# Gathered token rows turned on VectorE and moved within SBUF, in place of TensorE transposes

## The reference, cut to what matters

```python
x = x + attention(layernorm(x), ctx)            # 32 heads, 8 groups; not touched
h = layernorm(x).reshape(T, 512)                 # T = 8 * 256 = 2048 tokens
logits = h @ gate_w.T                            # 32 experts, the best 4 of each token
cw[t, sel] = softmax weights of the best 4, normed to 1
g = einsum('th,ehi->eti', h, Wg); u = einsum('th,ehi->eti', h, Wu)
a = silu(g) * u * cw.T[:, :, None]
large = einsum('eti,eih->th', a, Wd)             # inner width 192
small = the same with cWg, cWu, cWd: 16 chunks, inner width 128, chunk = expert // 2
out = x + large + 0.05 * small
```

## Time and profile before

| | |
|---|---|
| median of 3 runs | 1080.85 us |
| profiled execution, its own time | 1079.25 us |
| its span | 1077.5 us |
| TensorE busy | 1005.4 us (93%) |
| ScalarE / VectorE / GpSimd busy | 374.5 / 415.3 / 298.5 us |
| expert stage, first gather to the end | 458.8 to 1077.5 us |
| one slot in it, start to start | 7.65 us |
| DMA engines busy in it | 65 to 70% |

### The profile page before, as it was taken

The page is one execution under the profiler, slowest core; times in us unless marked ns, Lnnn a source line. Parts: engine busy times, 40 slices in busy tenths (PEclk is TensorE's granted clock), DMA queues, the critical chain, the costliest instruction groups (busy, mean ns, idle before and its releaser), DMA issues.

```text
span 1077.5 us, 18627 instructions
## 1 busy us (share of the span) xinstructions
PE 1005.4 (93%) x5447; PEld 651.7 (60%) x5448; DVE 415.3 (39%) x1065; ACT 374.5 (35%) x730; POOL 298.5 (28%) x395
## 2 busy tenths in 40 slices
PE   8889999999999877279999999999999999999995
PEld 6566667666665534156666666666666666666662
DVE  5587777777776627711111111111111111111110
ACT  2255454554555637812122222222222222222221
POOL 3011101011020002123434343433343434343442
PEclk9899999999999988579999999999999999999998
DMA  6163324243231118017566676766676677667433
GB/s 215 39 159 94 80 58 110 72 105 87 68 94 44 41 67 335 10 44 224 150 157 186 191 214 165 211 164 208 157 203 171 150 225 214 160 155 219 80 61 60
DMA packets 51755, 146.68 MB, mean 136 GB/s; under 512 B 9856, under 2 KB 19200, under 8 KB 47360
## 3 DMA queue, kind: packets, MB, share of 16 engines
q1 hardware_dynamic: 32016, 103.11, 29.1%
q0 software_dynamic: 17632, 42.74, 20.3%
q10 hardware_dynamic: 2064, 0.26, 0.2%
HBM read 100.73 MB, written 29.36 MB: 121 GB/s over the span
## 4 chain that ended last, share of the span: by engine, by line
PE 55%; DMA 1%; issue 0%; ACT 0%; POOL 0%; DVE 0%; POOLq 0%; ACTq 0%
PE y_ps L1564 18%; PE g_ps L1547 16%; PE u_ps L1547 16%; PE xt_ps L1540 3%; PE at_ps L1556 2%; DMA out_x<-yb,yidx 0%; DMA xg<-xd,gidx 0%; POOL out_x L1451 0%; ACT yb L1483 0%; ACT xT L1472 0%; ACT sg L1476 0%; DVE a L1518 0%; DVE a L1519 0%; POOL gidx L1434 0%; POOLq L1458 0%
## 5 line engine op out<-in xcount | busy, mean ns | idle before, releaser
L1564 PE MATMUL y_ps<-W,aT 128*128 x468 | 213.8, 593 | 0.8 <-DVE aT L1505 0.8
L1451 POOL DMA_INDIRECT out_x<-yb,yidx x78 | 125.3, 1606 | 296.0 <-DMA out_x<-yb,yidx 120.2
L397 ACT ACTIVATE pt<-stp 128x512 f32<-128x512 f32 x256 | 139.1, 596 | 145.2 <-PE stp L723 144.4
L518 DVE TENSOR_REDUCE mx<-s 128x2 f32<-128x512 f32 x256 | 163.7, 682 | 59.5 <-PE s L709 58.8
L1547 PE MATMUL g_ps<-W,xT 128*128 x624 | 183.2, 437 | 0.9 <-ACT xT L1472 0.9
L1547 PE MATMUL u_ps<-W,xT 128*128 x624 | 181.0, 433 | 0.0
L1547 PEld LDWEIGHTS u_ps<-W,xT 128*128 128x128 f32 x624 | 118.9, 191 | 49.8 <-issue 0.6
L1518 DVE TENSOR_TENSOR a<-u_ps,sg 128x192 f32<-128x192 f32 x78 | 27.9, 358 | 291.1 <-ACT sg L1476 291.1
L1476 ACT ACTIVATE sg<-g_ps 128x320 f32<-128x320 f32 x78 | 34.1, 437 | 305.0 <-PE u_ps L1547 305.0
L1547 PEld LDWEIGHTS g_ps<-W,xT 128*128 128x128 f32 x624 | 113.5, 192 | 39.0 <-issue 2.4
L1564 PEld LDWEIGHTS y_ps<-W,aT 128*128 128x128 f32 x468 | 82.8, 190 | 75.6 <-issue 75.6
(11 more groups left out here) (188 smaller groups left out, 929.8 us busy)
## 6 DMA issues: line engine op xcount, KB each, us to landing
W<-in_wts SPq DMA_DIRECT2D x32, 2048.0 KB, 8.1
qst<-q SPq DMA_DIRECT2D x42, 256.0 KB, 5.0
xs<-in_x SPq DMA_DIRECT2D x8, 512.0 KB, 3.7
ctxT<-in_ctx SPq DMA_DIRECT2D x8, 512.0 KB, 4.1
out_x<-xs SPq DMA_DIRECT2D x16, 256.0 KB, 2.2
kst<-k SPq DMA_DIRECT2D x48, 64.0 KB, 2.1
xd<-xs SPq DMA_DIRECT2D x11, 256.0 KB, 2.6
qst<-nm SPq DMA_DIRECT2D x128, 2.0 KB
```

The source lines that it names most:

```text
L397: act.activation(pt[g % 2][:, 2 * (j % 2) + r, :, :], stp[n % STP][:, :, :], ACT.Exp, scale=DH ** -0.5).then_inc(exp_done, 1)
L518: dve.tensor_reduce(mx[j // CH % 2][:, h:2 * G:G], s1[r][:, :, :], AX.X, ALU.max)\
L1451: pool.indirect_dma_start(out[:, :], bass.IndirectOffsetOnAxis(yidx[p][:, :], 0), yb[p][:, :], None, compute_op=ALU.add).then_inc(y_added, ...
L1564: m = pe.matmul(y_ps[:, :], aT[p][:, c, :], W[:, bass.ds(buf, 1), GW + c * D:GW + (c + 1) * D].rearrange("p a d -> p (a d)"), start=(c == ...
```

## The change

The gathered rows no longer pass through TensorE. VectorE turns the 128 x 512 block in 32 x 32 pieces (`turn`, one instruction from `xg` into a new buffer `xb`, with the elements written at a step of two floats), and four DMAs issued by ScalarE's queue (`x_move`), one for each group of 32 tokens, bring the pieces to their partitions in `xT`. Each of them moves 64 KB from 32 partitions (2 KB each) to 128 partitions in runs of 64 floats (256 bytes): 256 runs a DMA, 1024 a slot. `xT` has another layout, in which two feature chunks alternate, so that `gate_up` reads its stationary operand at a step of two floats; the weights' rows are permuted on the host to fit. The token's weight is applied in `gated` (two products with a per-partition factor, in place of a product and a product with a constant), with a second column `wt[:, 1]` = 0.05 times the weight. `y_evac` becomes a plain copy. `xt_ps` is gone.

The order also changes: gathers run four slots ahead instead of two, and behind `add` instead of ahead of it; `turn` of slot s+2 stands behind `gated` of slot s on VectorE; `x_move` of slot s+2 stands behind `y_evac` of slot s-1 on ScalarE, and waits for `turned` and for the products of slot s (`gu_full`).

```diff
             def gather(s, p):
-                    pool.wait_ge(xt_full, s - 1)
-                    pool.wait_ge(wt_ready, s - 1)
+                    pool.wait_ge(turned, s - 1)
...
                     for p in range(2):
-                        gather(i * 2 + p + 2, p)
                         add(i * 2 + p - 1, 1 - p)
+                        gather(i * 2 + p + 4, p)
...
-            def x_evac(s, p):
-                act.wait_ge(xt_full, s + 1)
-                act.copy(xT[p][:, :, :], xt_ps[p][:, :].rearrange("p (c t) -> p c t", c=C)).then_inc(xt_empty, 1)
+            def x_move(s, p):
+                act.wait_ge(turned, s + 1)
+                if not (isinstance(s, int) and s < 2):
+                    act.wait_ge(gu_full, s - 1)
+                for i in range(QB):
+                    act.dma_start(xT[p][:, :, i * Q:(i + 1) * Q, :].rearrange("m h r l -> m h (r l)"),
+                                  xb[p][i * Q:(i + 1) * Q, :]).then_inc(x_ready[p], DMA)
...
-                act.wait_ge(wt_ready, s + 1)
-                act.activation(yb[p][:, :], y_ps[:, :], ACT.Copy, scale=wt[p][:, :]).then_inc(y_empty, 1)
+                act.copy(yb[p][:, :], y_ps[:, :]).then_inc(y_empty, 1)
             def slot(s, p, first=False):
                 silu(s, p)
-                x_evac(s + 1, 1 - p)
                 if not first:
                     y_evac(s - 1, 1 - p)
+                x_move(s + 2, p)
...
+            def turn(s, p):
+                weights_of(s, p)
+                if not (isinstance(s, int) and s < 2):
+                    dve.wait_ge(x_ready[p], moved(s - 2, p))
+                dve.transpose(xb[p][:, :].rearrange("p (h r l) -> p h l r", r=Q, l=2), xg[p][:, 0:D]).then_inc(turned, 1)
             def gated(s, p):
-                weights_of(s, p)
                 dve.wait_ge(sg_ready, s + 1)
-                dve.tensor_tensor(a[p][:, 0:IL], u_ps[p][:, 0:IL], sg[p][:, 0:IL], ALU.mult)
-                dve.scalar_tensor_tensor(a[p][:, IL:IW], u_ps[p][:, IL:IW], SMALL, sg[p][:, IL:IW], ALU.mult,
+                dve.scalar_tensor_tensor(a[p][:, 0:IL], u_ps[p][:, 0:IL], wt[p][:, 0:1], sg[p][:, 0:IL], ALU.mult,
+                                         ALU.mult)
+                dve.scalar_tensor_tensor(a[p][:, IL:IW], u_ps[p][:, IL:IW], wt[p][:, 1:2], sg[p][:, IL:IW], ALU.mult,
                                          ALU.mult).then_inc(a_ready, 1)
...
             def gate_up(s, p, buf):
-                pe.wait_ge(xt_empty, s + 1)
+                pe.wait_ge(x_ready[p], moved(s, p))
...
-                        m = pe.matmul(ps_[p][:, 0:IW], xT[p][:, c, :],
+                        m = pe.matmul(ps_[p][:, 0:IW], xT[p][:, c // 2, :, c % 2],
...
                 gate_up(s, p, buf)
-                transpose_x(s + 1, 1 - p)
```

More of the change, by code:

```diff
@@ L966 @@
 SMALL = 0.05
+Q = 32
+QB = P // Q
 NW = 4
@@ L1305, in _ @@
                               ALU.add).then_inc(id4_ready, 1)
[L1306 to L1308 removed]
+            dve.memset(tok[:, NS:NS + 4], 0)
+            dve.memset(slot_e[:, NS:NS + 4], 0)
+            dve.memset(slot_buf[:, NS:NS + 4], 0)
             dve.wait_ge(root_ready, 1)
@@ L1382, in experts @@
         xg = [sb(f"xg{i}", [P, XW], F32) for i in range(2)]
-        wt = [sb(f"wt{i}", [P, 1], F32) for i in range(2)]
-        xT = [sb(f"xT{i}", [P, C, P], F32) for i in range(2)]
+        wt = [sb(f"wt{i}", [P, 2], F32) for i in range(2)]
+        xb = [sb(f"xb{i}", [P, D], F32) for i in range(2)]
+        xT = [sb(f"xT{i}", [P, C // 2, P, 2], F32) for i in range(2)]
         sg = [sb(f"sg{i}", [P, IW], F32) for i in range(2)]
@@ L1388, in experts @@
         yb = [sb(f"yb{i}", [P, D], F32) for i in range(2)]
-        xt_ps = [ps(f"xt_ps{i}", [P, 512]) for i in range(2)]
         g_ps = [ps(f"g_ps{i}", [P, 512]) for i in range(2)]
@@ L1396, in experts @@
         idx_ready, x_loaded = sem("idx_ready"), [sem(f"xg_loaded{i}") for i in range(2)]
-        xt_full, xt_empty, gu_full = sem("xt_full2"), sem("xt_empty2"), sem("gu_full")
+        turned, gu_full = sem("turned"), sem("gu_full")
+        x_ready = [sem(f"x_ready{i}") for i in range(2)]
         wt_ready = sem("wt_ready")
@@ L1403, in experts, with moved @@
         block = ctx.enter_context(nc.Block())
+        def moved(s, p):
+            return (s - p) * (QB * DMA // 2) + QB * DMA
         @block.sync
@@ L1455, in _ @@
                 gather(s, s % 2)
+            gather(4, 0)
             add(0, 0)
+            gather(5, 1)
             n, last = count(pool)
@@ L1465, in _ @@
             for p in range(2):
-                pool.wait_ge(x_loaded[p], n * DMA + DMA)
+                pool.wait_ge(x_loaded[p], n * DMA + 2 * DMA)
         @block.scalar
         def _(act):
-            def x_evac(s, p):
-                act.wait_ge(xt_full, s + 1)
-                act.copy(xT[p][:, :, :], xt_ps[p][:, :].rearrange("p (c t) -> p c t", c=C)).then_inc(xt_empty, 1)
+            def x_move(s, p):
[5 more added lines that the diff above has]
+                                  xb[p][i * Q:(i + 1) * Q, :]).then_inc(x_ready[p], DMA)
             def silu(s, p):
@@ L1499, in _ @@
             y_evac(last + 1, 1)
+            for p in range(2):
+                act.wait_ge(x_ready[p], n * (QB * DMA) + QB * DMA)
+                act.sem_inc(passed, 1)
         @block.vector
@@ L1523, in _ @@
                 dve.memset(a[p][:, IW:IP], 0.0)
+            turn(0, 0)
+            turn(1, 1)
             gated(0, 0)
+            turn(2, 0)
             at_evac(0, 0)
             gated(1, 1)
+            turn(3, 1)
             n, last = count(dve)
@@ L1532, in _ @@
                         gated(i * 2 + p, p)
+                        turn(i * 2 + p + 2, p)
             at_evac(last + 1, 1)
@@ L1536, in _ @@
         def _(pe):
-            def transpose_x(s, p):
-                pe.wait_ge(x_loaded[p], (s - p) * (DMA // 2) + DMA)
-                for c in range(C):
-                    m = pe.transpose(xt_ps[p][:, c * P:(c + 1) * P], xg[p][:, c * P:(c + 1) * P], ident[:, :])
-                m.then_inc(xt_full, 1)
             def gate_up(s, p, buf):
-                pe.wait_ge(xt_empty, s + 1)
+                pe.wait_ge(x_ready[p], moved(s, p))
                 for ps_, g in ((g_ps, 0), (u_ps, 1)):
                     for c in range(C):
-                        m = pe.matmul(ps_[p][:, 0:IW], xT[p][:, c, :],
+                        m = pe.matmul(ps_[p][:, 0:IW], xT[p][:, c // 2, :, c % 2],
                                       W[:, bass.ds(buf, 1), (2 * c + g) * IW:(2 * c + g + 1) * IW]
@@ L1600, in build @@
         gw, gw_loaded = sb("gw", [P, C, E_], F32), ctx.enter_context(nc.semaphore("gw_loaded"))
-        tabs = (sb("tok", [P, NS + 2], U32), sb("dst", [P, NS], U32), sb("slot_e", [P, NS + 2], I32),
-                sb("slot_buf", [P, NS + 2], I32), sb("cum_i", [P, E_], I32), sb("turns", [P, 2], I32))
+        tabs = (sb("tok", [P, NS + 4], U32), sb("dst", [P, NS], U32), sb("slot_e", [P, NS + 4], I32),
+                sb("slot_buf", [P, NS + 4], I32), sb("cum_i", [P, E_], I32), sb("turns", [P, 2], I32))
         w_loaded = [ctx.enter_context(nc.semaphore(f"w_loaded{i}")) for i in range(NW)]
```

13 lines of the change are left out of this document (8 added, 5 removed).

## The result

The changed kernel takes 1234.44 us (median of 4 runs, 1231.39 to 1237.0), the kernel before 1081.26 us on the same chip (4 runs, 1080.56 to 1083.21). The ratio is 1.142, with a 95% interval of 1.139 to 1.145: the change costs 153 us. The prediction was 1177 us, with a range up to 1228, so the sign was right and the moves were late behind every load, as forecast, but the price was too small: the time lies 6 us above the range.

The account below looks back on a forecast made before the run. TensorE was taken to bound the expert stage. The sum 1079.25 - 33.5 + 3.7 + 89.6 + 36.4 = 1175.45, with runs 1.6 us above the profile, gave 1177 us; range 1049 to 1228, the forecast's own 1100 to 1228.

Parts of the forecast that it names:

- What bounds, what is saved: Expert stage is one row of TensorE work; dropping the x transposes saves 78 x 0.43 = 33.5 us, slot 7.22 us.
- VectorE: Block transposition on VectorE takes 0.7 us a slot and, with the changed product in gated, costs nothing.
- The issues: Four move issues on ScalarE take 2.75 us, 0.69 each, ending before silu is due; an undisturbed slot pays nothing.
- The stride: Gate products' stationary operand read at a step of two floats: nothing taken; other bound 125 us.
- The start: First gate products of the expert stage wait for turn and moves: 3.7 us more, 2.5 to 6 allowed.
- The moves beside a load: Moves issued behind a weight load land 3.2 us late for the gate products: 28 x 3.2 = 89.6 us.
- the upper bound of T + 13.1: Moves also stand behind the gather, landing 13.1 us after the slot's activation transposes start (T), 5.5 us late.
- the lower bound: Moves land right behind the load with only their own 0.85 us of data after it, 1.75 us late.
- Small transfers behind a load stand still until it is through.: On the DMA engines, moves issued behind a 2 MB load wait until it is through, as the scatter-add did.
- the rule that the prediction cited: Each DMA engine alternates packets between queues with work, so moves would slip between the load's packets.
- the first rival: Moves get turns beside the load on the DMA engines, mostly landing in time: 1051 us, faster; chance 0.20.
- The clock: TensorE's clock falls behind waits for moves, costing 1.7 us in three of four cases: 28 x 1.3 = 36.4 us.

Follow-up runs that it names:

- e1_no_loads: The changed kernel without the 28 expert weight loads of the expert stage, the first four experts' weights being used again: 1054.91 us, ratio 0.977.
- e6_no_adds: The changed kernel without the scatter-adds and the waits for them, so expert results are not added to the output: 1146.39 us, ratio 1.062.
- e7_two_moves: The changed kernel with only two of the four moves of each slot, 64 of 128 tokens of xT staying zero: 1196.6 us, ratio 1.111.
- e2_fine_loads: The changed kernel with each 2 MB weight load made of 1 KB pieces in place of 16 KB rows: 1246.2 us, ratio 1.153.
- e12_gaps: The kernel before, with TensorE waiting in each odd slot ahead of its gate products for a VectorE fill of 3584 columns: 1347.36 us, ratio 1.247.
- e10_early_halves: The changed kernel with turn ahead of gated, moves right behind silu, gather ahead of add, and each load in two halves a slot apart: 1054.83 us, ratio 0.976.
- e4_moves_early: The changed kernel with the block transposition ahead of the gated product and the moves right behind silu, load unmoved: 1131.98 us, ratio 1.047.

## Why the prediction was right, and where it was wrong

Two terms of the sum were too small: the lateness of the moves behind a load (89.6 us taken, 124.8 measured) and the clock behind it (36.4 taken, 53.3 measured). The range did not cover them, because its upper end did not use the prediction's own bounds.

- **What bounds, what is saved.** Right. The undisturbed slot is 7.22 us, as worked out from two starts in the earlier trace rows.
- **VectorE.** Right. The block transposition took 707 ns where 0.7 us was taken; nobody waits for it in the loop.
- **The issues.** Right: 2.6 to 2.9 us for four, where 2.75 was taken from the earlier trace rows. They start before `y_evac` has ended (819.91 against 819.77 + 0.58).
- **The stride.** Right: taking nothing was correct. A stationary load takes 197 ns in `e1_no_loads`, where the clock is full, against 191 in the earlier trace rows; the 204 of the changed kernel contains the loads at half the clock. The groups of both kernels (line, engine, operation, count, busy us, mean ns, idle time before), first that of `e1_no_loads`, with the block transposition of the changed kernel at the end:

```profile
L1569 PEld LDWEIGHTS u_ps<-W,xT 128*128 128x128 f32 x624 | 123.0, 197 | 45.8 <-issue 0.6
```

```profile
L1571 PEld LDWEIGHTS u_ps<-W,xT 128*128 128x128 f32 x624 | 127.4, 204 | 51.1 <-issue 8.8
...
L1538 DVE STREAM_TRANSPOSE xb<-xg 128x512 f32<-128x512 f32 x80 | 56.6, 707 | 0.0
```

- **The start.** The gate products begin at 469.10 against 464.44 in the earlier trace rows: 4.7 us, where 3.7 was taken and 2.5 to 6 allowed. The fourth move landed 3.3 us after its issue there, not 2.1.
- **The end.** Not in the sum at all. From the start of the last slot with gate products to the end of the run the kernel before takes 23.3 us, the changed one 26.3, though one group of transposes is gone: 3.4 us more. The last down product waits 3.4 us for `aT` where it waited 0.75, and then runs at half the clock. Why VectorE copies the last `aT` so late, at 1218.02, no run shows.
- **The moves beside a load.** This is the term that was mis-sized. All 28 loads caused a wait, each in the slot after the load's issue, as foreseen. But the moves are late by 4.46 us on average (4.30 of recorded wait and 0.16), not 3.2: 28 x 4.46 = 124.8 us instead of 89.6. The landing was set equal to the add's, T + 10.7. That choice took the nearest transfer by time of issue and forgot that four moves of 256-byte pieces are the longest row of pieces among the small transfers. They land at T + 12.0, behind the gather, near the upper bound of T + 13.1. `e6_no_adds` and `e7_two_moves` show what stood in the way: 1.7 us of adds, and about 1.6 us of the moves' own pieces, where the lower bound had 0.85 and the chosen value none that was its own.
- **"Small transfers behind a load stand still until it is through."** Wrong in that form. From 4.6 us after the load's issue the moves take turns with it, piece by piece, which is the rule that the prediction cited. Part of the add's silence in the earlier trace rows was no standing still either: without a load (`e1_no_loads`) its first packet comes 2.2 us after its issue, behind a load 4.8. By the Trainium skill, "DMA: Bandwidth & Descriptors", section "Queues, rings and completion order", an engine alternates between the queues that have work, and drains a whole packet, typically 9 to 17 descriptors, before it changes over. The trace agrees with the turns from 824.4 on (53 records of q10 beside 50 of q1) and not before it. Of the bundles it shows nothing: the records of the profile, which this text calls packets, alternate one for one, and in `e2_fine_loads` too (366 beside 370). The turns did not help as the first rival had it, because that rival gave a whole 64 KB move one turn, while each of the 64 pieces on an engine needs a turn of its own.
- **The clock.** Too small. The sum took a fall of 1.7 us in three of four cases. It fell in 28 of 28, seven times for twice as long: 53.3 us instead of 36.4. The earlier trace rows had both lengths and one wait of 1.85 us, from which the share of falls could not be known. `e6_no_adds`, `e7_two_moves` and `e12_gaps` give it: 8 of 28 behind waits of 2.6 us, 21 of 28 behind 3.5 us, 28 of 28 behind 4.3 us, 39 of 39 behind 4.5 us. The two errors are one chain: the longer wait also made the fall certain.

- **The range.** Its upper end was built from 4.2 us of lateness and 2.1 us of clock for each load, 6.3 us. Neither number is worked out; the prediction's own upper bounds were 5.5 and 3.4 us, and with them the range would have reached about 1300. The runs give 6.4 us a load (179.5 / 28), 3 us more in all, and without any load disturbing it the kernel takes 1054.91 us, not 1051: together they put the result above the range.

With the measured terms the same sum reads 1079.25 - 33.5 + 4.7 + 3.4 + 124.8 + 53.3 = 1232.0 us, against 1234.33 us of the profiled execution.

## What to carry to other kernels

A transfer that has a due time must not be issued just behind a large one that has none: price it by when its last piece lands behind everything already under way, counting its own pieces, not by the time of a neighbour. Put the large transfer behind the urgent ones, or move these ahead, by as long as they need to land and not only to be issued: with a lead of 2.6 to 2.9 us, where four moves need 4.2, the last pieces were still caught. And cut the large one in parts; `e10_early_halves` turned 1.142 into 0.976 with the same bytes. And price a gap of TensorE as the gap and the slower work behind it: here 4.5 us of standing still cost 6.4 to 6.8 us.

## What the runs showed of the hardware

- The moves, issued 0.1 us behind a 2 MB load, showed no packet for 4.6 to 4.9 us behind 27 of the 28 loads (4.3 behind the first). In `e1_no_loads` the first came 1.3 us after the issue. With the load in pieces of 1 KB it was 3.7 to 4.1 us (4.5 behind the first). What holds it was not found.
- After that the queues take turns, one record for one (53 beside 50; 366 beside 370 in `e2_fine_loads`), so a transfer of many small pieces is last. Issued 2.6 us ahead of a load, its last pieces can still be caught: in `e4_moves_early` 64 pieces went beside 109 rows of the load in 5 us.
- A piece of 256 bytes within SBUF costs an engine 0.018 to 0.020 us, between the 13 ns of 128 bytes and the 28 ns of 512 bytes of the earlier trace rows.
- The share of waits that are followed by the lower clock rises from 8 of 28 to 28 of 28 between waits of 2.6 and 4.3 us for late DMAs. Behind gaps of 4.5 us made by VectorE it is 39 of 39.
- A stationary operand read at a step of two floats costs nothing here: the slot stayed at 7.22 us.
